# Attention scores in three f32r passes instead of one f32 matmul, with q split on ScalarE and VectorE

## The chip, the cores and the metric

The kernel runs on one core of one Trainium2 chip. The metric is the device time of one execution in microseconds; smaller is better.

## The reference

The input x has 2 sequences of 2048 tokens with 512 values each, and ctx has 2 x 77 tokens of 512. The layer is a cross attention followed by a feed forward part, each with a residual:

```
xn = layernorm(x)
q, k, v = xn @ Wq.T + bq, ctx @ Wk.T + bk, ctx @ Wv.T + bv      # 16 heads of 32
scores = q k^T / sqrt(32), with key s masked for token t where s > t
x = x + (softmax(scores) @ v) @ Wo.T + bo
xn = layernorm(x)
gate, up = fp4(xn) @ fp4(w_gate).T, fp4(xn) @ fp4(w_up).T        # 1408 values each
x = x + fp4(silu(gate) * up) @ fp4(w_down).T
```

`fp4` takes blocks of 16 values, scales each to its largest and rounds to the grid 0, 0.5, 1, 1.5, 2, 3, 4, 6 and back. All inputs are float32, and the rounding to the grid makes the result sensitive to small errors ahead of it. So most products are made with split operands: a high half that f32r (a rounded float32 that TensorE takes in one pass) holds exactly, and a low half that is the rest. `split_matmuls` (L170 to L178) adds high x high, high x low and low x high.

## The kernel before

A tile is 128 tokens; there are 32. The kernel has two stages, attention for all tiles, then feed forward for all tiles, and no engine needs another core. Each of the five engines has its own program; they meet through semaphores, whose waits are written out by hand, and so is the order of steps on each engine. Nothing is planned at run time: an engine that waits holds up all that stands behind it in its program.

In the attention stage, `iteration(a, n)` stands once for each engine. It works on tile a and the two before it (a - 1, a - 2), and beside them on one of 33 pieces n of the feed forward weights: it is rounded to fp4, turned and split there, 11 pieces of w_gate, 11 of w_up (kept in SBUF as `wguh`, `wgul`), and 11 of w_down, which go to DRAM through the outgoing buffer `wd_out`. Pieces from number 3 on are turned by DMA: SyncE's queue transposes the grid values (`grid_transposed`, L497), stores the block scales (L491), loads them back spread over partitions with eight DMAs (`scales_in`, L504), and GpSimd multiplies (`scale_turned`, L586). `piece_high` on ScalarE (L867) and `piece_low` on VectorE (L1028) split the result. `store_piece` (L485) sends a down piece away, after `scales_in` in the order of SyncE's queue. Before, `wd_out` has two places, and a new piece waits for the store of the last but one.

Order of the steps around the change, in one iteration:

- TensorE: q of tile a in 12 f32r passes (`project_q`), transposes of att, probabilities, q and xn, the output matmuls of tile a - 2 in 12 passes, the scores of tile a, probabilities times v of tile a - 1, one transpose of scales.
- ScalarE: copy of q (L850), high half of att (L844), copies of the turned probabilities (L881), `shift` of piece n (L146), high half of xn (L888), 16 exps with the negative maxima as bias (L898), `piece_high`, rows of scales (L873).
- VectorE: largest of each block, low half of att (L963), scale, inverse and negative inverse of the piece, `q_bias` (L970), `piece_low`, rounding of the piece (L151, L155), low half of xn, grid values (L1033), residual (L982), maxima of the scores (L990), norm statistics, normalised att, normalised x (L1017).
- GpSimd: division of the piece (L140), `scale_turned`, norm scalars, addition of the output bias (L570).

The scores of a tile are 16 heads of 77 keys in three PSUM banks. The keys stand in `kbd` as a block diagonal of four heads, so five matmuls do, of 4, 2, 2, 4 and 4 heads: 308, 154, 154, 308 and 308 columns, in plain f32 with `qt`, the turned q with its bias, as the stationary operand (L764). A first tile of a sequence adds the mask with a bf16 matmul ahead of each.

The first tile and the setup (all before about 50 us) are written out: Wk, Wq, Wv, Wo are loaded and turned, `keys()` on VectorE fills `kbd` with eight steps on 32 partitions (L1112), `values` makes `vext` (v with a column of ones), and SyncE's queue places it in the block diagonal `vbd` with 24 DMAs (L538), before it goes on to the pieces.

## Time and profile before

| | us |
|---|---|
| median of 3 runs | 1179.34 (1178.81 to 1179.55) |
| time of the profiled execution | 1178.53 |
| its span | 1176.7 |
| TensorE matmuls busy | 1158.8 (98%) |
| VectorE busy | 970.3 (82%) |
| ScalarE busy | 483.5 (41%) |
| GpSimd busy | 179.3 (15%) |
| granted TensorE clock, mean | 0.999 |

The span goes from the first to the last instruction of the profiled execution; its own time has 1.8 us around that. Times in the trace count from the start of the span. A row in order of time has the start, the duration, the engine, the line of the kernel, the operation, output and inputs by name, shapes, and how many instructions are merged in it; in brackets stands idle time of the engine before it and what ended it. PE is TensorE, PEld its weight loads, DVE VectorE, ACT ScalarE, POOL GpSimd, SPq the queue of SyncE. Matmuls overlap each other in the pipeline, so a busy TensorE isn't at its peak, and start to start is the measure of its pace. A plain f32 matmul shows as two records, an f32r pass as one. Rows of DMA issues show the time of the issue; the landing comes later.

### The profile page before, as it was taken

To read this page: it belongs to the slowest core of one execution; us is meant where nothing else is said; L and a number is where in the kernel's file an instruction comes from. 1 tells how busy PE (TensorE), PEld (TensorE's weight loads), DVE (VectorE), ACT (ScalarE), POOL (GpSimd) and SP (SyncE) were. 2 spreads that over 40 slices of the span, in tenths; PEclk is the share of its full clock that TensorE was granted. 3 is DMA by queue.
4 is the path that set the end of the run, shared out by engine and by line. 5 is a ranking of instruction groups with operands and counts; after the bars stand their busy time and mean duration, and the time that the engine had idled before them with its cause. 6 is when DMAs were issued, how large, how long until landed. Compare 5 with 4: busy or idle time off the path is not lost.

```text
span 1176.7 us, 21716 instructions
## 1 busy us (share of the span) xinstructions
PE 1158.8 (98%) x6784; PEld 1057.6 (90%) x6784; DVE 970.3 (82%) x1609; ACT 483.5 (41%) x1201; POOL 179.3 (15%) x305
## 2 busy tenths in 40 slices
PE   7899999999999999999999999999999999999998
PEld 6688888888888889999999999999999999999997
DVE  6778888888888877988888888888888888888865
ACT  3556656566566553333332332233233323333321
POOL 3433333333333310000000000000000000000000
PEclk9999999999999999999999999999999999999999
DMA  7223323323344436554445345444534454453442
GB/s 240 45 89 88 111 88 110 91 84 111 108 139 148 132 108 194 150 105 86 89 89 102 70 93 99 88 88 87 105 70 93 98 90 88 82 104 76 82 85 46
DMA packets 154955, 119.30 MB, mean 101 GB/s; under 512 B 95597, under 2 KB 122301, under 8 KB 154660
## 3 DMA queue, kind: packets, MB, share of 16 engines
q1 hardware_dynamic: 154916, 118.85, 42.7%
q8 instruction: 16, 0.26, 0.1%
q14 instruction: 23, 0.19, 0.1%
HBM read 74.47 MB, written 24.94 MB: 84 GB/s over the span
## 4 chain that ended last, share of the span: by engine, by line
PE 78%; SPq 7%; DMA 7%; DVE 2%; ACT 2%; issue 2%; POOL 2%; POOLq 0%; DVEq 0%; ACTq 0%
PE g_ps L175 7%; PE u_ps L175 7%; PE u_ps L176 7%; PE g_ps L176 7%; PE u_ps L177 7%; PE g_ps L177 7%; PE d_ps L1436 6%; PE d_ps L1437 6%; PE d_ps L1435 6%; SPq L504 4%; DMA ws_dram<-w_rows 4%; PE o_ps L784 3%; PE s_ps L764 3%; DMA w_wide<-ws_dram 3%; POOL w_q L586 2%
## 5 line engine op out<-in xcount | busy, mean ns | idle before, releaser
L175 PE MATMUL g_ps<-wguh,xnh 128*128 128x352 f32 x496 | 162.4, 327 | 0.5 <-issue 0.5
L175 PE MATMUL u_ps<-wguh,xnh 128*128 128x352 f32 x496 | 159.9, 322 | 0.5 <-DVE hid L1576 0.5
L176 PE MATMUL u_ps<-wgul,xnh 128*128 128x352 f32 x496 | 159.8, 322 | 0.0
L176 PE MATMUL g_ps<-wgul,xnh 128*128 128x352 f32 x496 | 159.8, 322 | 0.0
L177 PE MATMUL u_ps<-wguh,xnl 128*128 128x352 f32 x496 | 159.6, 322 | 0.0
L177 PE MATMUL g_ps<-wguh,xnl 128*128 128x352 f32 x496 | 159.5, 322 | 0.0
L898 ACT ACTIVATE probs<-s_ps,nsmax 128x77 f32<-128x77 f32 x512 | 113.7, 374 | 92.2 <-DVE nsmax L990 92.2
L1576 DVE TENSOR_TENSOR hid<-u_ps,silu 128x352 f32<-128x352 f32 x128 | 66.8, 522 | 78.1 <-PE u_ps L177 75.8
L1437 PE MATMUL d_ps<-wd,hql 128*128 128x512 f32 x330 | 128.9, 391 | 0.0
L1436 PE MATMUL d_ps<-wd,hqh 128*128 128x512 f32 x330 | 128.9, 391 | 0.0
L1435 PE MATMUL d_ps<-wd,hqh 128*128 128x512 f32 x330 | 128.4, 389 | 0.0
L1478 ACT ACTIVATE silu<-g_ps 128x352 f32<-128x352 f32 x128 | 58.4, 460 | 134.0 <-PE g_ps L177 134.0
L274 POOL TENSOR_TENSOR nmean<-f_mv,minus_one 128x1 f32<-128x1 f32 x32 | 6.1, 190 | 630.8 <-DVE f_mv L269 630.8
L175 PEld LDWEIGHTS g_ps<-wguh,xnh 128*128 128x128 f32 x496 | 93.1, 188 | 2.6 <-issue 0.9
L146 ACT ACTIVATE quant_magic<-quant_z 128x512 bf16<-128x512 f32 x65 | 41.0, 631 | 132.2 <-DVE quant_z L140 79.5
L176 PEld LDWEIGHTS g_ps<-wgul,xnh 128*128 128x128 f32 x496 | 93.2, 188 | 1.1
L175 PEld LDWEIGHTS u_ps<-wguh,xnh 128*128 128x128 f32 x496 | 93.1, 188 | 0.8 <-DVE hid L1576 0.8
L177 PEld LDWEIGHTS u_ps<-wguh,xnl 128*128 128x128 f32 x496 | 93.4, 188 | 0.0
L177 PEld LDWEIGHTS g_ps<-wguh,xnl 128*128 128x128 f32 x496 | 93.4, 188 | 0.0
L176 PEld LDWEIGHTS u_ps<-wgul,xnh 128*128 128x128 f32 x496 | 93.2, 188 | 0.0
L784 PEld LDWEIGHTS o_ps<-vbd,probsT 128*128 128x128 f32 (+1 forms) x640 | 76.5, 191 | 4.4
L784 PE MATMUL o_ps<-vbd,probsT 128*128 128x66 f32 (+2 forms) x640 | 75.0, 272 | 0.0
(175 smaller groups left out, 2547.1 us busy)
## 6 DMA issues: line engine op xcount, KB each, us to landing
scale_wide<-st_dram SPq DMA_DIRECT2D x248, 88.0 KB, 3.4
xin<-in_x_dram SPq DMA_DIRECT2D x32, 256.0 KB, 2.8
x_dram<-x SPq DMA_DIRECT2D x32, 256.0 KB, 2.2
xin<-x_dram SPq DMA_DIRECT2D x32, 256.0 KB, 2.7
out_dram<-y SPq DMA_DIRECT2D x32, 256.0 KB, 2.1
scale_wide<-st_dram SPq DMA_DIRECT2D x248, 32.0 KB, 1.8
w_wide<-ws_dram SPq DMA_DIRECT2D x240, 32.0 KB, 1.9
wd_dram<-wd_out SPq DMA_DIRECT2D x11, 512.0 KB, 3.0
```

The costliest lines, as they stand in the source:

```text
L146: s.activation(self.magic[:, part.cols], self.z[:, part.cols], ACT.Copy, scale=ULP_SHIFT).then_inc(self.shifted_ready, 1)
L175: pe.matmul(out, lh, rh, start=(i == 0), stop=False)
L176: pe.matmul(out, lh, rl, start=False, stop=False)
L177: last = pe.matmul(out, ll, rh, start=False, stop=(i == n - 1))
L504: sp.dma_start(w_wide[b * BLK:(b + 1) * BLK, :, :], ws_dram[:, b, :].unsqueeze(0).to_broadcast([BLK, EC, P])).then_inc(w_wide_loaded, 16)
L784: last = pe.matmul(o_ps[:, half, h0 * VW:(h1 + 1) * VW], probsT[0:rows, i, :], vbd[0:rows, b, half, c, 0:(h1 - h0 + 1) * VW], start=(c == ...
L898: last = act.activation(probs[:, h * CTX:(h + 1) * CTX], s_ps[:, bank, o:o + CTX], ACT.Exp, bias=nsmax[:, h:h + 1], scale=1.0)
L1435: pe.matmul(total, high[:, c, :], wd[:, 0, c, :], start=(c == 0), stop=False)
L1436: pe.matmul(total, high[:, c, :], wd[:, 1, c, :], start=False, stop=False)
L1437: summed = pe.matmul(total, low[:, c, :], wd[:, 0, c, :], start=False, stop=(c == FC - 1))
L1478: act.activation(silu[:, c % 2, :], g_ps[:, c % 2, 0:GU_N], ACT.Silu).then_inc(silu_ready, 1)
L1576: dve.tensor_tensor(hid[:, c * GU_N:(c + 1) * GU_N], u_ps[:, c % 2, 0:GU_N], silu[:, c % 2, :], ALU.mult).then_inc(hid_ready, 1)
```

## The change

The keys are kept as a high and a low half, `kbh` and `kbl`, and q as `qh` and `ql`, all f32r. Each of the five score matmuls becomes three passes. On ScalarE, `q_high` makes the high half in four biased copies of 128 columns out of PSUM, after the copies of the turned probabilities and ahead of `shift`. On VectorE, `q_low` makes the low half in four steps, and stands behind `piece_low`, where `q_bias` stood ahead of it. TensorE waits for both. In the setup VectorE makes the whole keys `kf` in one step, ScalarE copies them into `kbh` in eight steps ahead of the first q copy, and VectorE subtracts in eight steps to `kbl` ahead of the first `q_low`. The places of both must be zeroed, one more memset on GpSimd. In SBUF, `wd_out` has one place, `vext` and `kf` lie in rows that only the setup uses, and q lies under `ql`.

```diff
-        kbd = sb("kbd", [P, B, EC, 4 * CTX])
+        kbh, kbl = sb("kbh", [P, B, EC, 4 * CTX], F32R), sb("kbl", [P, B, EC, 4 * CTX], F32R)
...
-        q = sb("q", [P, E])
-        qt = sb("qt", [P, EC, P])
+        with ExitStack() as qctx:
+            q = qctx.enter_context(nc.sbuf_tensor("q", [P, E], F32))
+        ql = sb("ql", [P, EC, P], F32R)
+        qh = sb("qh", [P, EC, P], F32R)
...
-        wd_out = sb("wd_out", [P, 2, 2, E], F32R)
+        wd_out = sb("wd_out", [P, 2, E], F32R)
...
-            pool.memset(kbd[:], 0.0).then_inc(zeroed, 1)
+            pool.memset(kbh[:].bitcast(F32), 0.0).then_inc(zeroed, 1)
+            pool.memset(kbl[:].bitcast(F32), 0.0).then_inc(zeroed, 1)
...
             def scores(a):
-                pe.wait_ge(q_ready, a + 1)
+                pe.wait_ge(qh_ready, a + 1)
+                pe.wait_ge(ql_ready, a + 1)
...
-                    last = pe.matmul(out, qt[:, c, :], kbd[:, b, c, (h0 % 4) * CTX:(h0 % 4 + h1 - h0) * CTX],
-                                     start=not causal, stop=True)
+                    cols = slice((h0 % 4) * CTX, (h0 % 4 + h1 - h0) * CTX)
+                    pe.matmul(out, qh[:, c, :], kbh[:, b, c, cols], start=not causal, stop=False)
+                    pe.matmul(out, qh[:, c, :], kbl[:, b, c, cols], start=False, stop=False)
+                    last = pe.matmul(out, ql[:, c, :], kbh[:, b, c, cols], start=False, stop=True)
...
+            def q_high(t):
+                act.wait_ge(qT_done, t + 1)
+                if reached(t):
+                    act.wait_ge(s_done, S_BANKS * t)
+                for c in range(EC):
+                    last = act.activation(qh[:, c, :], q_ps[:, c * P:(c + 1) * P], ACT.Identity, bias=bqc[:, c:c + 1], scale=1.0)
+                last.then_inc(qh_ready, 1)
...
                 if down:
                     c = n - GU_PIECES
-                    if isinstance(c, int) and c >= 2:
-                        act.wait_ge(wd_stored, 16 * (c - 1))
-                    if not isinstance(c, int):
-                        act.wait_ge(wd_stored, 16 * (c - 1))
-                    dst = wd_out[:, c % 2, 0, :].rearrange("p (c k) -> p c k", k=P)
+                    if reached(c):
+                        act.wait_ge(wd_stored, 16 * c)
+                    dst = wd_out[:, 0, :].rearrange("p (c k) -> p c k", k=P)
...
                 if valid(a - 1):
                     probs_copy(a - 1)
+                if valid(a):
+                    q_high(a)
...
+            def keys():
+
+                act.wait_ge(kf_ready, 1)
+                act.wait_ge(zeroed, 2)
+                for b in range(B):
+                    for i in range(4):
+                        r = slice(i * HD, (i + 1) * HD)
+                        last = act.activation(kbh[r, b, :, i * CTX:(i + 1) * CTX], kf[r, :, b * CTX:(b + 1) * CTX], ACT.Copy)
+                last.then_inc(kbh_ready, 1)
...
             wquant.shift(act, 1)
+            keys()
             q_copy(0)
             weight_high(2)
+            q_high(0)
...
-            def q_bias(t):
-                dve.wait_ge(qT_done, t + 1)
+            def q_low(t):
+                dve.wait_ge(qh_ready, t + 1)
                 if reached(t):
                     dve.wait_ge(s_done, S_BANKS * t)
-                dve.tensor_tensor(qt[:], q_ps[:].rearrange("p (c k) -> p c k", k=P), bcast(bqc[:], P), ALU.add).then_inc(q_ready, 1)
+                for c in range(EC):
+                    last = dve.scalar_tensor_tensor(out=ql[:, c, :], in0=q_ps[:, c * P:(c + 1) * P], scalar=bqc[:, c:c + 1],
+                                                    in1=qh[:, c, :].bitcast(F32), op0=ALU.add, op1=ALU.subtract)
+                last.then_inc(ql_ready, 1)
...
-                if valid(a):
-                    q_bias(a)
                 if by_dma(n - 2):
                     piece_low(n - 2, down)
+                if valid(a):
+                    q_low(a)
...
-                for b in range(B):
-                    for i in range(4):
-                        r = slice(i * HD, (i + 1) * HD)
-
-                        last = dve.scalar_tensor_tensor(
-                            out=kbd[r, b, :, i * CTX:(i + 1) * CTX],
-                            in0=kp[r].rearrange("p a (c s) -> p (a c) s", c=2)[:, :, b * CTX:(b + 1) * CTX],
-                            scalar=SCALE, in1=bcast(bkc[r, :], CTX), op0=ALU.mult, op1=ALU.add)
-                last.then_inc(kbd_ready, 1)
+                dve.scalar_tensor_tensor(out=kf[:], in0=kp[:].rearrange("p a (c s) -> p (a c) s", c=2)[:, :, 0:B * CTX],
+                                         scalar=SCALE, in1=bcast(bkc[:], B * CTX), op0=ALU.mult,
+                                         op1=ALU.add).then_inc(kf_ready, 1)
+
+            def keys_low():
+
+                dve.wait_ge(kbh_ready, 1)
+                for b in range(B):
+                    for i in range(4):
+                        r = slice(i * HD, (i + 1) * HD)
+                        cols = slice(i * CTX, (i + 1) * CTX)
+                        last = dve.tensor_tensor(kbl[r, b, :, cols], kf[r, :, b * CTX:(b + 1) * CTX],
+                                                 kbh[r, b, :, cols].bitcast(F32), ALU.subtract)
+                last.then_inc(kbl_ready, 1)
...
             piece_rounded(0)
-            q_bias(0)
+            keys_low()
+            q_low(0)
             piece_scales(1)
```

## Rows read from the trace of the kernel before

**Rows 1.** Busy us (x instructions) by window: PE, PEld, DVE, ACT, POOL; clock, DMA, GB/s.
```profile
92.00:240.00 148.00, 147.76 (x926) 129.09 (x925) 126.56 (x267) 91.46 (x305) 50.97 (x61) 1.00 0.33 98
...
290.00:414.00 124.00, 124.00 (x774) 108.69 (x773) 104.90 (x220) 77.39 (x254) 42.57 (x53) 1.00 0.43 134
```

**Rows 2.** Waits, 60 to 430 us: total us, times, longest.
```profile
ACT q L850 <- PE q_ps L177: 4.1, 14, 1.0
```

**Rows 3.** The chain that ended last, 300 to 327 us, by line.
```profile
by line: DMA ws_dram<-w_rows 22.5%; DMA w_wide<-ws_dram 21.6%; SPq L504 21.3%; SPq L497 13.4%; POOL w_q L586 13.1%; issue 6.4%; SPq L463 3.9%; SPq L457 3.1%; SPq L477 2.9%; POOLq L585 0.4%; POOLq L563 0.2%; SPq L496 0.2%; SPq L462 0.1%; SPq
```

**Rows 4.** TensorE in order of time, 209 to 213 us: start us, us, engine, line.
```profile
208.99 2.24 PE L764 MATMUL s_ps<-kbd,qt 128*128 128x308 f32 x10
211.07 2.34 PE L784 MATMUL o_ps<-vbd,probsT 128*128 128x66 f32 x20
```

**Rows 5.** ScalarE in order of time, 89 to 102 us.
```profile
89.18 3.56 ACT L898 ACTIVATE probs<-s_ps,nsmax 128x77 f32<-128x77 f32 x16 [2.95 <-DVE nsmax L990]
...
94.14 1.37 ACT L881 ACTIVATE probsT<-s_ps 128x512 f32<-128x512 f32 x3
...
97.19 0.63 ACT L146 ACTIVATE quant_magic<-quant_z 128x512 bf16<-128x512 f32 x1 [1.69 <-POOL quant_z L140]
...
101.26 3.12 ACT L898 ACTIVATE probs<-s_ps,nsmax 128x77 f32<-128x77 f32 x14 [2.95 <-DVE nsmax L990]
```

**Rows 6.** VectorE in order of time, 94 to 98 us.
```profile
94.38 0.69 DVE L963 TENSOR_TENSOR atl<-w_ps,ath 128x512 fp32r<-128x512 f32 x1 [1.08 <-ACT ath L844]
...
95.58 0.18 DVE L134 TENSOR_SCALAR quant_ninv<-quant_inv 128x32 f32<-128x32 f32 x1
95.77 0.69 DVE L970 TENSOR_TENSOR qt<-q_ps,bqc 128x512 f32<-128x512 f32 x1
96.38 1.33 DVE L1028 TENSOR_TENSOR wgul<-w_q,wguh 128x512 f32 x1
97.86 0.29 DVE L151 TENSOR_SCALAR quant_magic<-quant_magic 128x512 int16<-128x512 int16 x1
```

**Rows 7.** GpSimd, then VectorE, in order of time.
```profile
83.48 1.61 POOL L140 TENSOR_TENSOR quant_z<-w_in,quant_ninv 128x512 f32<-128x512 f32 x1 [3.00 <-DVE quant_ninv L134]
...
96.10 1.06 POOL L140 TENSOR_TENSOR quant_z<-w_in,quant_ninv 128x512 f32<-128x512 f32 x1 [1.99 <-DVE quant_ninv L134]
...
83.49 0.68 DVE L1028 TENSOR_TENSOR wgul<-w_q,wguh 128x512 f32 x1
```

**Rows 8.** TensorE in order of time, 620 us: f32r passes of 352 columns.
```profile
620.11 0.32 PE L177 MATMUL u_ps<-wguh,xnl 128*128 128x352 f32 x1
...
620.27 0.32 PE L175 MATMUL u_ps<-wguh,xnh 128*128 128x352 f32 x1
```

**Rows 9.** The line that stores down pieces; ScalarE in order of time.
```profile
L485 SPq DMA_DIRECT2D wd_dram<-wd_out x11: 520/538/638, 311.7 to 431.1; - x11
DMA to landing us min/median/max: 3.0/3.0/4.6
...
314.70 0.66 ACT L867 ACTIVATE wd_out<-w_q 128x512 f32 x1
```

**Rows 10.** The start, in order of time: VectorE, ScalarE, TensorE, SyncE's queue, GpSimd.
```profile
19.74 3.90 DVE L1112 SCALAR_TENSOR_TENSOR kbd<-kp,bkc 32x308 f32<-32x308 f32 x8 [0.45 <-PE kp L670]
...
20.46 0.63 ACT L146 ACTIVATE quant_magic<-quant_z 128x512 bf16<-128x512 f32 x1 [4.28 <-POOL quant_z L140]
22.53 0.60 ACT L850 ACTIVATE q<-q_ps 128x512 f32<-128x512 f32 x1 [1.43 <-PE q_ps L177]
23.02 2.06 ACT L940 ACTIVATE wvt<-tp 128x512 f32<-128x512 f32 x4
...
25.14 3.66 PE L679 MATMUL o_ps<-wvt,ctxT 128*77 128x512 f32 x8 [0.36 <-ACT wvt L940]
...
29.67 20.57 SPq L538 DMA_DIRECT2D vbd<-vext  x24
...
9.05 0.19 POOL L564 TENSOR_TENSOR veps<-mv,eps 128x1 f32<-128x1 f32 x1 [3.30 <-DVE mv L1011]
```

More of the change, by code:

```diff
@@ L200, in __init__ @@
             self.wkt, self.wvt = row(("wkt", [P, EC, E]))[0], row(("wvt", [P, EC, E]))[0]
-            self.cin, self.ctxT = row(("cin", [CTX, B, E]), ("ctxT", [P, EC, B, CTX]))
-            self.bv_all, self.bias_nat = row(("bv_all", [CTX, E]), ("bias_nat", [EC, 2, P]))
+            self.cin, self.ctxT, self.kf = row(("cin", [CTX, B, E]), ("ctxT", [P, EC, B, CTX]), ("kf", [P, EC, B * CTX]))
+            self.bv_all, self.bias_nat, self.vext = row(
+                ("bv_all", [CTX, E]), ("bias_nat", [EC, 2, P]), ("vext", [CTX, B, 2, HALF_HEADS, VW]))
 class Shared:
@@ L354, in attention @@
         mask = sb("mask", [P, CTX], BF16)
-        vext = sb("vext", [CTX, B, 2, HALF_HEADS, VW])
         wqh, wql = sb("wqh", [P, EC, E], F32R), sb("wql", [P, EC, E], F32R)
@@ L377, in attention @@
         w_nat, wkt, wvt, cin, ctxT = k.setup.w_nat, k.setup.wkt, k.setup.wvt, k.setup.cin, k.setup.ctxT
-        bv_all, bias_nat = k.setup.bv_all, k.setup.bias_nat
+        bv_all, bias_nat, vext, kf = k.setup.bv_all, k.setup.bias_nat, k.setup.vext, k.setup.kf
         with ExitStack() as sctx:
@@ L405, in attention @@
         small_done, small_ready = sem("small_done"), sem("small_ready")
-        k_done, kbd_ready = sem("k_done"), sem("kbd_ready")
+        k_done, kf_ready, kbh_ready, kbl_ready = sem("k_done"), sem("kf_ready"), sem("kbh_ready"), sem("kbl_ready")
         v_done, v_ready = sem("v_done"), sem("v_ready")
@@ L415, in attention @@
         xnT_done, xnh_ready, xnl_ready = sem("xnT_done"), sem("xnh_ready"), sem("xnl_ready")
-        q_done, q_copied, qT_done, q_ready = sem("q_done"), sem("q_copied"), sem("qT_done"), sem("q_ready")
+        q_done, q_copied, qT_done, qh_ready, ql_ready = (sem(n) for n in (
+            "q_done", "q_copied", "qT_done", "qh_ready", "ql_ready"))
         s_done, nsmax_ready, probs_ready = (sem(n) for n in ("s_done", "nsmax_ready", "probs_ready"))
@@ L484, in store_piece @@
                     sp.wait_ge(wd_stored, 16 * c)
-                sp.dma_start(wd_dram[:, :, c, :], wd_out[:, c % 2].bitcast(F32)).then_inc(wd_stored, 16)
+                sp.dma_start(wd_dram[:, :, c, :], wd_out[:].bitcast(F32)).then_inc(wd_stored, 16)
             def scales_out(n):
@@ L530, in sp_part @@
             sp.wait_ge(const_ready, 3)
-            sp.wait_ge(zeroed, 2)
+            sp.wait_ge(zeroed, 3)
             for b in range(B):
@@ L685, in project_q @@
                 if reached(a):
-                    pe.wait_ge(q_ready, a)
+                    pe.wait_ge(qh_ready, a)
+                    pe.wait_ge(ql_ready, a)
                 else:
@@ L754, in scores @@
                 if not reached(a):
-                    pe.wait_ge(kbd_ready, 1)
+                    pe.wait_ge(kbh_ready, 1)
+                    pe.wait_ge(kbl_ready, 1)
                 b = a // TB
@@ L1023, in piece_low @@
                     c = n - GU_PIECES
-                    high, low = (wd_out[:, c % 2, i, :].rearrange("p (c k) -> p c k", k=P) for i in range(2))
+                    high, low = (wd_out[:, i, :].rearrange("p (c k) -> p c k", k=P) for i in range(2))
                 else:
@@ L1105, in keys @@
                 dve.wait_ge(k_done, 1)
-                dve.wait_ge(zeroed, 1)
                 dve.wait_ge(small_ready, 3)
+                dve.scalar_tensor_tensor(out=kf[:], in0=kp[:].rearrange("p a (c s) -> p (a c) s", c=2)[:, :, 0:B * CTX],
[3 more added lines that the diff above has]
+                dve.wait_ge(kbh_ready, 1)
                 for b in range(B):
@@ L1175, in dve_part @@
             run(dve, iteration, 1)
-        over = Over(q_done, q_ready, pT_ready, att_ready, wo_done, x1_ready, xb_ready)
+        over = Over(q_done, ql_ready, pT_ready, att_ready, wo_done, x1_ready, xb_ready)
         return Parts(sp_part, pool_part, pe_part, act_part, dve_part), over
```

## Prediction

> **What bounds the kernel now.** I read the busy times by window first. The change lies in the attention stage, which ends at about 430 us of 1176.7. There TensorE is listed as busy all the time, VectorE 85%, ScalarE 62%, GpSimd 34% [rows 1]. One tile makes 77 matmul records (12 for q, 12 for the output, 10 scores, 20 probabilities by v, 23 transposes). So 926 records in 148 us are 12.0 tiles of about 12.33 us, and 774 in 124 us are 10.05 of the same 12.33.
>
> A full TensorE is not yet a TensorE that bounds, so I looked for loops that return to themselves without it. There are two, and both are nearly as long.
>
> The first I call the vector loop: exps, piece high, rows of scales, q copy and high half of att on ScalarE; low half of att, then scale, inverse and its negative on VectorE; division on GpSimd; shift on ScalarE; rounding, residual and maxima on VectorE; exps again. From 89.18 to 101.26 it takes 12.08 us [rows 5]. Its one steady wait for TensorE, at the q copy, is only 4.1 us in 14 cases over 370 us, some 30 tiles [rows 2]; this tile has none. So this loop has about 0.25 us of slack against 12.33.
>
> The second I call the transfer loop: transposed grid, store, loads, scales out and landed, eight scale loads and landed, GpSimd's product, next transpose. In the stage of the down pieces the chain that ended last runs through it almost alone: scales out 22.5%, scales in 21.6%, their issues 21.3%, transpose 13.4%, GpSimd's product 13.1% [rows 3]. There a faster TensorE buys nothing.
>
> **The change, part by part.**
>
> *Scores.* Before, the ten records of the five f32 matmuls take from 208.99 to 211.07, 2.08 us for 1232 columns, 1.69 ns a column [rows 4]. After, each of the five is three f32r passes: nine of 308 columns and six of 154. The nearest f32r row is 352 columns at 0.16 us from start to start [rows 8]; at full speed, 2.4 GHz, the columns are 0.147 of it, so 0.013 is overhead. A pass of 308 is then 0.141. For 154 no f32r row exists. Bounds: the same arithmetic gives 0.077; the f32 rate of rows 4 gives 0.26. I take 0.11, which is what one of the 20 short records of probabilities by v takes (2.18 us in all, up to the next piece: 2.34 less the overlap of about 0.16 that the scores' row shows too) [rows 4]. Sum: 9 x 0.141 + 6 x 0.11 = 1.93, saving 0.15 a tile. Ends: 1.73 (saves 0.35) and 2.83 (costs 0.75). TensorE's own loop becomes 12.18 us.
>
> *q's halves.* ScalarE is free at 94.14 + 1.37 = 95.51 and shifts at 97.19 [rows 5]; the four biased copies go in there. A step of 77 columns with a bias costs 3.56 / 16 = 0.22 [rows 5], one of 512 columns 2.06 / 4 = 0.51 [rows 10]. I take 0.28 for 128 columns (nearer to the 77), so 1.1 to 1.2 for four, with ends 0.9 and 2.0: the high half is there at 96.7. That is within the hole. VectorE had its bias step at 95.77 and the piece's low half at 96.38 [rows 6]; the two change places. Four low steps start at 96.75. One costs between 0.2 (the 0.18 us step of 32 columns [rows 6] with its gap) and 0.49 (3.90 / 8 for 308 columns [rows 10]). I take 0.26, near the low end because only 128 columns stream, so 1.05 for four: ready at 97.8, with 0.8 and 2.0 as ends. The rounding waits for ScalarE's shift at 97.86 anyway [rows 6], so the four steps are covered by 0.1 to 0.3 us, no more. Behind them on VectorE stand rounding, xn low, residual and maxima, and all ScalarE waits for the maxima. TensorE's twelve output matmuls begin when att's low half is there, at 94.38 + 0.69 [rows 6], and take 12 x (0.213 + 0.013) = 2.7, so to 97.8: the scores hardly wait.
>
> *The low half of the piece comes earlier, and that has a price.* At 96.38 it took 1.33 us because GpSimd was dividing; where it began within 0.01 us of the division it took 0.68 and GpSimd needed 1.61 instead of 1.06 as at 96.10, ending at 85.09, 0.92 after VectorE's step ended at 84.17 [rows 7]. Now the step starts at 95.77, 0.3 us ahead of GpSimd's 96.10, and ends at 96.46. By the same 0.92 the division ends at 97.38; before, it ended just ahead of the shift at 97.19 [rows 5]. So shift and rounding move by 0.22 us, and the vector loop goes from 12.08 to 12.30. Bounds: nothing (the division is not held up), or 0.55 (it is held up in full).
> The Trainium skill ("SBUF — State Buffer", the section on the engine ports) says VectorE and GpSimd share a port pair that is an exclusive lock for the whole instruction for two-SBUF-input steps, whoever starts first. Rows 7 agree in both directions (1.33 and 1.61). By it the hand-over cannot be free, which speaks against the change.
> The Trainium skill ("ScalarE: Activation LUTs", what ACT_TABLE_LOAD costs) adds 93 ns for each pointer operand; by its figures an estimate for the four copies is 1.27 us instead of 1.2. No row has 128 columns with a bias.
>
> So for tiles 4 to 20: TensorE 12.18, vector loop 12.30, transfers just below. The largest is 12.30 against 12.33: 16 x 0.03 = 0.5 us gained, practically nothing. TensorE's saving goes into the wait of the output matmuls for att's low half.
>
> *One outgoing buffer.* It touches 10 of the 11 down pieces. The store is issued after the eight scale loads, the first one at 311.7, and lands 3.0 us later (4.6 at worst), that is at 314.7; the next piece's high half now writes the same buffer and started at 314.70 [rows 9]. Until now it had a tile more. So landing and need fall together. I price one late landing of 4.6 at 1.0 and the rest at 0.05 each: 1.5 us, ends 0 and 3. Behind this wait on ScalarE stand the scale rows and the q copy, then att's high half, for which VectorE and TensorE wait. In that stage the transfer loop sets the pace, so TensorE's gain gives nothing back.
>
> *The start.* VectorE's eight key steps (3.90 us from 19.74 [rows 10]) become one of 616 columns (about 0.8, by 0.49 for 308) and eight subtractions (3.2 to 3.9). ScalarE gets eight copies of 308 columns ahead of the q copy: 0.34 each (between 0.22 and 0.51), 2.7 us, and they can't begin before the shift ends at 20.46 + 0.63 = 21.09. So the q copy goes from 22.53 to 23.75, wv's copies and the value matmuls (25.14) follow by 1.2 [rows 10]. VectorE can begin the subtractions at 23.8; with the low half of q and the next scales it arrives at the values at about 30.1. SyncE's queue of 24 placements of v, 20.57 us long, starts at 29.67 as soon as v is there [rows 10], and moves by 1.2 too. I add 0.2 for tile 1, where the halves of q are late for TensorE by about 1 us before it has slack: 1.4, ends 0.5 and 2.5. A second memset of 2 us on GpSimd lies in the 3.3 us that it idles before 9.05 [rows 10] and costs nothing; without that cover it would be 2. New places of vext and kf in memory cost nothing.
>
> Sum: +1.4 - 0.5 + 1.5 = +2.4, and the first score tile -0.1, gives +2.3. On the profiled execution (span 1176.7, time 1178.53) that is 1180.8; the median of the runs is 0.8 above it, 1179.34, so 1181.6.
>
> **The rivals.**
> *A. TensorE's gain passes through.* The lock costs nothing and ScalarE's copies at the start hide behind the wait for TensorE. Then 32 x 0.15 = 4.8 us come off, 1174.5. For it: TensorE busy 100%. Against it: rows 3, and a slack of only 0.25. It decides if the vector loop stays below 12.18.
> *B. Narrow passes don't get the f32r rate.* Six of 154 columns at 0.26: scores take 2.83, TensorE's loop 13.08, 32 x 0.75 = +24 us, 1203. For it: no f32r row under 352 columns in the trace. Against it: short f32 records go at 0.11. It decides from 0.135 a narrow pass (scores no cheaper than 2.08).
> *C. The small steps cost more.* 0.1 us more for each of the eight: the low half is there at 98.6 instead of 97.8, 0.5 after the shift, vector loop 12.8; 27 tiles x 0.47 = +12.7, 1194. It decides when both sets together pass 98.1. For it: thin cover; against: rows of short steps (0.18 to 0.22).
> *D. The change doesn't do what it says*: nothing in the code speaks for that; the third pass is there in each group.
>
> **How the numbers follow.** The forecast and what lies close around it (1178 to 1186, by the ends of start, landing and lock) gets 0.55, A 0.2, B 0.13, C 0.12. A change of under 0.2%, 2.4 us, can't be told from none here. The forecast lies at that edge, so its 0.55 goes 0.28 to no change and 0.27 to slower. Faster: A, 0.2. Slower: B, C and the rest, 0.52. The range takes in A and most of C and leaves B out: 1174.5 to 1192.
>
> **What would show it.** Fifteen score records a tile, spanning 1.9 us; a pass of 154 columns near 0.11. The low half of the piece at 0.7 and GpSimd's division at 1.3. VectorE idle less than 0.3 before the rounding. TensorE waiting before the output matmuls. ScalarE waiting for the store in some down pieces. Tiles of 12.3 us in both windows, and v's placements from about 31. The forecast is wrong if tiles are under 12.2 or over 12.5, or if the start moves by more than 2.5.

## The result, and the profile after

| | before | changed |
|---|---|---|
| median, us | 1179.27 (1178.81 to 1182.34, 8 runs) | 1188.3 (1184.23 to 1189.33, 8 runs) |
| profiled execution, its span | 1178.53, 1176.7 | 1188.65, 1186.7 |
| TensorE, VectorE busy | 1158.8, 970.3 | 1164.4, 974.8 |
| ScalarE, GpSimd busy | 483.5, 179.3 | 516.6, 189.6 |
| mean granted clock | 0.999 | 0.992 |

The ratio is 1.0066, with a 95% interval of 1.005 to 1.0082: slower, by 9.0 us in the medians and 10.1 between the profiled executions. The forecast said slower by 2.3, and its range held the time.

The loss is spread very unevenly. This table follows fixed points of the program through both traces, in us from the start of the span:

| point | before | changed | later by |
|---|---|---|---|
| first maxima of tile 0 | 32.16 | 35.20 | 3.0 |
| q copy, tile 1 | 45.24 | 48.73 | 3.5 |
| first score, tile 1 | 48.13 | 52.85 | 4.7 |
| q copy, tile 2 | 55.66 | 64.79 | 9.1 |
| q copy, tile 3 | 67.91 | 76.97 | 9.1 |
| q copy, last tile | 414.38 | 423.68 | 9.3 |
| first gate group of the FFN | 427.76 | 437.48 | 9.7 |

So 9.1 of some 10 us are lost before 65 us, and the 29 tiles after that lose next to nothing. Half of the 9.1 is lost in one tile, and there TensorE's clock is the thing to look at. Busy time by window of the changed kernel, with the columns of [rows 1]; the column of one number behind POOL is the granted clock:

```profile
42.30:45.70 3.40, 3.40 (x11) 2.83 (x12) 2.54 (x6) 1.11 (x2) 1.83 (x2) 0.50 0.11 16
45.70:52.60 6.90, 4.38 (x29) 3.27 (x27) 3.55 (x10) 3.83 (x10) 2.12 (x2) 0.99 0.12 17
52.60:62.80 10.20, 9.95 (x41) 9.60 (x42) 7.10 (x16) 4.47 (x19) 1.35 (x3) 0.50 0.28 70
62.80:73.00 10.20, 10.20 (x71) 9.30 (x69) 6.09 (x15) 4.80 (x13) 2.89 (x3) 1.00 0.09 26
92.00:240.00 148.00, 148.00 (x986) 133.56 (x986) 124.96 (x301) 101.57 (x350) 55.36 (x61) 1.00 0.32 97
290.00:414.00 124.00, 123.42 (x823) 111.51 (x823) 104.51 (x252) 85.19 (x291) 45.08 (x51) 1.00 0.42 129
```

From 42.3 to 45.7 and from 52.6 to 62.8 the clock was the lower of its two levels, 1.2 GHz. The kernel before had it only from 11.3 to 14.7; the changed one has that early stretch too, from 11.6 to 15.0. In the second stretch TensorE is busy 9.95 of 10.20 us and gets through 41 records; the next 10.20 us hold 71. Ahead of the stretch it was busy 4.38 of 6.90 us. In the two lower windows, 986 records against 926 in rows 1: tiles have 82 records instead of 77, and the clock is full.

TensorE in order of time: tile 1 of the kernel before, then of the changed kernel tile 1 and a later tile at full clock.

```profile
48.13 2.35 PE L764 MATMUL s_ps<-kbd,qt 128*128 128x308 f32 x10 [1.15 <-DVE qt L970]
...
49.87 0.60 PE L747 MATMUL xn_ps<-ident,xn 128*128 128x128 f32 x4
52.85 0.59 PE L773 MATMUL s_ps<-kbh,qh 128*128 128x308 f32 x1 [2.39 <-DVE ql L1001]
53.24 0.46 PE L774 MATMUL s_ps<-kbl,qh 128*128 128x308 f32 x1
...
56.58 4.37 PE L794 MATMUL o_ps<-vbd,probsT 128*128 128x66 f32 x20
...
217.40 0.30 PE L773 MATMUL s_ps<-kbh,qh 128*128 128x308 f32 x1
217.54 0.30 PE L774 MATMUL s_ps<-kbl,qh 128*128 128x308 f32 x1
217.69 0.31 PE L775 MATMUL s_ps<-kbh,ql 128*128 128x308 f32 x1
217.83 0.23 PE L773 MATMUL s_ps<-kbh,qh 128*128 128x154 f32 x1
...
218.24 0.28 PE L774 MATMUL s_ps<-kbl,qh 128*128 128x154 f32 x1
218.35 0.27 PE L775 MATMUL s_ps<-kbh,ql 128*128 128x154 f32 x1
218.46 0.34 PE L773 MATMUL s_ps<-kbh,qh 128*128 128x308 f32 x1
...
219.35 2.34 PE L794 MATMUL o_ps<-vbd,probsT 128*128 128x66 f32 x20
```

At full clock a pass of 308 columns takes 0.14 to 0.15 from start to start and one of 154 columns 0.11, and the scores 219.35 - 217.40 = 1.95 where rows 4 had 2.08. In tile 1 TensorE waits 2.39 us for q's low half, where the kernel before waited 1.15 for q, and then every record is long: 0.46 instead of 0.30, and the probabilities by v 4.37 instead of 2.34.

The middle tile of the changed kernel on ScalarE, VectorE and GpSimd, in order of time (it answers to rows 5, 6 and 7):

```profile
214.70 1.18 ACT L867 ACTIVATE qh<-q_ps,bqc 128x128 fp32r<-128x128 f32 x4
216.79 0.63 ACT L146 ACTIVATE quant_magic<-quant_z 128x512 bf16<-128x512 f32 x1 [0.92 <-POOL quant_z L140]
...
213.72 0.69 DVE L993 TENSOR_TENSOR atl<-w_ps,ath 128x512 fp32r<-128x512 f32 x1 [1.12 <-ACT ath L854]
...
215.15 0.69 DVE L1061 TENSOR_TENSOR wgul<-w_q,wguh 128x512 f32 x1
216.01 1.13 DVE L1001 SCALAR_TENSOR_TENSOR ql<-q_ps,bqc,qh 128x128 fp32r<-128x128 f32 x4 [0.17 <-ACT qh L867]
217.46 0.29 DVE L151 TENSOR_SCALAR quant_magic<-quant_magic 128x512 int16<-128x512 int16 x1 [0.32 <-ACT quant_magic L146]
...
215.34 1.42 POOL L140 TENSOR_TENSOR quant_z<-w_in,quant_ninv 128x512 f32<-128x512 f32 x1 [1.88 <-DVE quant_ninv L134]
```

The four copies take 1.18, the four low steps 1.13. The piece's low half is down from 1.33 to 0.69, and GpSimd's division is up from 1.06 to 1.42. VectorE idles 0.32 before the rounding. The next tile begins 12.33 later, as do nearly all tiles beside which a piece of w_gate or w_up is worked on; before, they alternated between 12.30 and 12.35. In the stage of the down pieces the tiles take 12.2 to 12.8. Of the waits of the changed kernel from 75 to 440 us:

```profile
ACT q L860 <- PE q_ps L177: 0.5, 2, 0.3
...
ACT wd_out L883 <- DMA wd_dram<-wd_out: 0.8, 3, 0.4
```

The first answers to rows 2: from there on the q copy hardly waits for TensorE now (3.8 us in 13 cases in the same window before). The vector loop has no slack left and sets the pace. The second is what ScalarE waits for the single outgoing buffer: 0.8 us in three pieces, where it waited 0.2 in one before. TensorE's saving turns into a wait, as forecast: in the tile above, its output matmuls start 0.51 us after the transposes of xn ahead of them (214.04 to 214.55), before it was 0.36 (205.77 to 206.13).

The start of the changed kernel, ScalarE and then VectorE (rows 10):

```profile
20.98 3.77 ACT L967 ACTIVATE kbh<-kf 32x308 fp32r<-32x308 f32 x8
24.77 0.60 ACT L860 ACTIVATE q<-q_ps 128x512 f32<-128x512 f32 x1
25.27 2.06 ACT L958 ACTIVATE wvt<-tp 128x512 f32<-128x512 f32 x4
...
19.76 0.80 DVE L1141 SCALAR_TENSOR_TENSOR kf<-kp,bkc 128x616 f32<-128x616 f32 x1 [0.49 <-PE kp L675]
...
24.78 3.87 DVE L1152 TENSOR_TENSOR kbl<-kf,kbh 32x308 fp32r<-32x308 f32 x8 [1.93 <-ACT kbh L967]
28.68 1.13 DVE L1001 SCALAR_TENSOR_TENSOR ql<-q_ps,bqc,qh 128x128 fp32r<-128x128 f32 x4
29.73 0.68 DVE L120 TENSOR_REDUCE quant_amax<-w_in 128x32 f32<-128x512 f32 x1
...
31.20 0.68 DVE L1161 TENSOR_TENSOR vext<-o_ps,bv_all 77x512 f32<-77x512 f32 x1
...
33.13 0.69 DVE L151 TENSOR_SCALAR quant_magic<-quant_magic 128x512 int16<-128x512 int16 x1 [0.29 <-ACT quant_magic L146]
...
35.20 1.56 DVE L1023 TENSOR_REDUCE nsmax<-s_ps 128x6 f32<-128x462 f32 x3
```

The last three of these steps in the kernel before:

```profile
28.90 0.69 DVE L1123 TENSOR_TENSOR vext<-o_ps,bv_all 77x512 f32<-77x512 f32 x1 [0.82 <-PE o_ps L679]
...
30.50 0.28 DVE L151 TENSOR_SCALAR quant_magic<-quant_magic 128x512 int16<-128x512 int16 x1
...
32.16 1.56 DVE L990 TENSOR_REDUCE nsmax<-s_ps 128x6 f32<-128x462 f32 x3
```

A key copy on ScalarE takes 0.47, and VectorE idles 1.93 for them. The step that makes v comes 2.3 later than before, the rounding 2.6 later, and the rounding takes 0.69 instead of 0.28, so that the maxima come 3.0 later.

### The profile page after: what moved, and what is told of

Same layout as the page of the kernel before. It is cut to its first block, busy times and chain, and to the rows that moved or that the text cites. A ratio compares the mean times of both kernels' runs of the same rounds, so it can differ in the third digit from the quotient of the medians.

```text
span 1186.7 us, 22287 instructions
## 1 busy us (share of the span) xinstructions
PE 1164.4 (98%) x6944; PEld 1073.5 (90%) x6944; DVE 974.8 (82%) x1706; ACT 516.6 (44%) x1337; POOL 189.6 (16%) x306
## 4 chain that ended last, share of the span: by engine, by line
PE 85%; DVE 3%; DMA 3%; ACT 3%; SPq 2%; issue 2%; POOL 1%; DVEq 0%; POOLq 0%; ACTq 0%
PE g_ps L175 7%; PE u_ps L175 7%; PE u_ps L176 7%; PE g_ps L176 7%; PE u_ps L177 7%; PE g_ps L177 7%; PE d_ps L1475 6%; PE d_ps L1476 6%; PE d_ps L1474 6%; PE o_ps L794 4%; PE s_ps L735 2%; PE w_ps L175 2%; PE q_ps L175 2%; PE w_ps L177 2%; PE w_ps L176 2%
```

## The experiments

Eleven kernels, each timed in five rounds against the kernel before. They ran in three groups; the kernel before had medians of 1179.92, 1180.57 and 1181.54 over the runs up to each, so the ratio is the measure, not the time alone. The two numbers behind a ratio are its 95% interval.

**One outgoing buffer, alone.** (e1_one_outgoing_buffer) The kernel before with one edit:

```diff
-        wd_out = sb("wd_out", [P, 2, 2, E], F32R)
+        wd_out = sb("wd_out", [P, 2, E], F32R)
...
+                    if reached(c):
+                        act.wait_ge(wd_stored, 16 * c)
```

> The kernel before with one outgoing buffer for the down pieces, and nothing else of the change. Theory (my term for it): a store lands when the next piece wants the buffer, so 1.5 us more, 0 to 3, ratio 1.000 to 1.0025, and one to three waits of ScalarE for the store in the stage of the down pieces. Rival: the single buffer carries a good part of the 9 us by which the changed kernel is slower: then 4 us or more, ratio over 1.0034.

Measured: 1180.78 us (1178.30 to 1181.63), ratio 1.000 [0.9989, 1.0011]. The profile has a span of 1177.6 against 1176.7, and ScalarE waits 1.0 us in all for the store (0.2 before). So the buffer costs between nothing and about 1 us.

**Two passes instead of three.** (e2_two_passes) The changed kernel without the product of q's high half with the keys' low half:

```diff
-                    pe.matmul(out, qh[:, c, :], kbl[:, b, c, cols], start=False, stop=False)
```

> The changed kernel with the pass qh x kbl left out of the scores, so five f32r passes a tile fewer; about 0.65 us less work for TensorE a tile, 20 us over 32 tiles. Theory (the vector loop sets the pace): the tiles in the middle stay at 12.33 us, the whole time falls by under 2 us, and TensorE waits about 0.65 us more a tile ahead of the output matmuls. Rival (TensorE sets it): tiles of 11.7 us, some 20 us less, about 1168.

Measured: 1187.18 (1185.38 to 1189.44), ratio 1.0067 [1.0052, 1.0082]. A third of the score passes is gone, and the time and the tiles of 12.33 us stay. In the middle of the attention stage TensorE isn't the limit any more.

**Idle matmuls in tile 1.** (e3_filler_matmuls) The changed kernel, with TensorE's waits of tile 1 filled by f32r passes whose result nobody reads:

```diff
+            def filler(n):
+                for _ in range(n):
+                    pe.matmul(w_ps[:], wqh[:, 0, 0:P], wqh[:, 1, :], start=True, stop=True)
...
                 if isinstance(a, int) and a == 1:
+                    pe.wait_ge(wth_ready, 4 * EC)
+                    pe.wait_ge(wtl_ready, 2 * EC)
+                    filler(8)
                     transpose_piece(2)
...
+                if isinstance(a, int) and a == 1:
+                    filler(10)
                 if valid(a):
                     scores(a)
```

> The changed kernel with 18 idle f32r matmuls of 512 columns, whose result nobody reads, in the two gaps that TensorE has in tile 1 (8 ahead of the turning of piece 2, 10 ahead of the scores). Theory: about 5 of the 9 us by which the changed kernel is slower are matmuls at 1.2 GHz between 52.4 and 62.7 us, after those gaps; with the gaps filled the granted clock is 0.999 in each run, and the median is 1183 to 1185. Rival: the late vector chain of the start costs the 9 us by itself: 1187 to 1189 as before.

Measured: 1186.02 (1183.18 to 1188.38), ratio 1.0055 [1.0039, 1.007]. The window from 52 to 58 us of its profile:

```profile
52.00:58.00 6.00, 5.90 (x41) 5.21 (x40) 5.22 (x14) 3.05 (x11) 1.06 (x1) 1.00 0.22 63
```

The long stretch at half clock is gone (the one at 42 isn't). The scores of tile 1 come 1.4 us later, because the filling is longer than the gap, and yet the q copy of tile 2 comes at 61.55 instead of 64.79. The median falls by 2.3 (by the ratios it is 1.3), less than the 3 to 5 that I expected, and the interval overlaps that of the changed kernel: the profile shows the effect, the times alone don't.

**Scales ahead of the key steps.** (e4_scales_first) The changed kernel, with one line moved in VectorE's start:

```diff
+            piece_scales(1)
             keys_low()
             q_low(0)
-            piece_scales(1)
```

> The changed kernel with the scales of piece 1 on VectorE moved ahead of the low half of the keys, into the 1.93 us in which VectorE waits for ScalarE's key copies. Theory (the start is bound by VectorE's chain): the first maxima come 1.4 us earlier, at 33.8 instead of 35.2, and the time falls by 1.4 us in runs of the same clock. Rival (the start is bound by ScalarE's copies and the value matmuls behind them): no change at the first exps.

Measured: 1183.72 (1182.04 to 1185.65), ratio 1.0035 [1.0022, 1.0047]. First maxima at 34.28 (35.20), first exps at 35.25 (35.86), exps of tile 1 at 54.34 (55.66). So 0.9 us is gained at the maxima, where 1.4 was expected, and 1.3 only in tile 1. The median is 4.6 lower (by the ratios 3.7), more than the 1.4 expected; this profile's stretch at half clock is 6.8 us instead of 10.2. Part of the gain is paid back: the key subtractions took 5.61 us instead of 3.87, beside GpSimd's division (1.22) and its addition of the output bias (1.50), which now run at the same time.

**The piece's low half first, alone.** (e5_low_first_alone) The kernel before, with the two steps exchanged on VectorE:

```diff
-                if valid(a):
-                    q_bias(a)
                 if by_dma(n - 2):
                     piece_low(n - 2, down)
+                if valid(a):
+                    q_bias(a)
```

> The kernel before with one edit: the low half of the piece ahead of the bias of q on VectorE. Theory (the lock on the shared port moves the division): GpSimd's division goes from 1.06 to 1.4, rounding comes 0.2 to 0.35 later, and the vector loop goes from 12.08 to about 12.35. TensorE's own loop is still 12.33 here, so a tile stays at 12.33 to 12.4 and the time rises by 0 to 2 us, ratio 1.000 to 1.0017, but the q copy no longer waits for TensorE. Rival (the division is not held up, or the loop has slack enough): division 1.06, no change at all.

Measured: 1181.73 (1180.62 to 1185.25), ratio 1.0009 [0.9999, 1.002]. GpSimd's division in its profile:

```profile
145.29 1.34 POOL L140 TENSOR_TENSOR quant_z<-w_in,quant_ninv 128x512 f32<-128x512 f32 x1 [1.97 <-DVE quant_ninv L134]
```

So the order alone makes the division 0.28 longer. Middle tiles are 12.35 (12.33), those of the down stage 12.48 (12.33).

**The piece's low half earlier still.** (e6_low_early) The changed kernel: outside the down stage the low half goes ahead of att's low half, well before the division, and GpSimd adds the output bias one tile later, out of its way. The edit to that addition isn't shown here.

```diff
...
+                if by_dma(n - 2) and not down:
+                    piece_low(n - 2, down)
                 if valid(a - 2):
                     att_low(a - 2)
...
-                if by_dma(n - 2):
+                if by_dma(n - 2) and down:
                     piece_low(n - 2, down)
```

> The changed kernel; outside the stage of the down pieces the low half of the piece stands ahead of att's low half, in VectorE's idle 1.1 us, and the addition of the output bias on GpSimd is made one tile later, behind the scaled product, so that it does not hold the port there. Theory (the lock costs the vector loop 0.25 to 0.35 us a tile): the division is back at 1.06, and tiles of the middle go from 12.33 to about 12.2 (TensorE's own 12.19), 16 x 0.13 = 2 us less than the changed kernel. Rival (something else holds 12.33, as the transfers): division at 1.06, but tiles stay at 12.3 and the time as it is.

Measured: 1187.64 (1184.61 to 1191.93), ratio 1.006 [1.0041, 1.008]. GpSimd's division and two starts of ScalarE's exps in its profile:

```profile
138.59 1.06 POOL L140 TENSOR_TENSOR quant_z<-w_in,quant_ninv 128x512 f32<-128x512 f32 x1 [3.83 <-DVE quant_ninv L134]
...
143.75 3.57 ACT L918 ACTIVATE probs<-s_ps,nsmax 128x77 f32<-128x77 f32 x16 [2.95 <-DVE nsmax L1027]
155.93 3.35 ACT L918 ACTIVATE probs<-s_ps,nsmax 128x77 f32<-128x77 f32 x15 [2.95 <-DVE nsmax L1027]
```

The division is back at 1.06 and the tile at 12.18, which is TensorE's own loop of the prediction. But one tile in about seven takes 12.8: in the one from 180.30 to 193.18 GpSimd's product waits 5.00 us for the scale loads, and VectorE idles 1.17 for the norm scalars that stand behind it. That fits a transfer loop slower than 12.18 that asks for its time back. No gain in the median is shown: the interval is nearly that of the changed kernel.

**Short key steps.** (e7_short_keys) The changed kernel with only one of the eight key copies and one of the eight subtractions; the other seven blocks of the keys are left at zero, so most of the scores are left out. The same edit stands in both places:

```diff
-                    for i in range(4):
+                    for i in range(1 - b):
```

> The changed kernel with one of the eight key copies on ScalarE and one of the eight subtractions on VectorE; the other seven blocks of the keys are left at zero. Theory (the start is lost in these 7 x 0.47 + 7 x 0.48 us): first maxima 4 to 5 us earlier than in the changed kernel, by 31 us, and the time is within 1.5 us of the kernel before or below it, 1177 to 1181, with no stretch of half clock after 50 us. Rival (the loss is in the loop or in tile 1's later halves of q): over 1184.

Measured: 1186.46 (1184.69 to 1188.95), ratio 1.0045 [1.0028, 1.0061]. The first exps came at 33.53, only 0.6 behind the kernel before. I had expected 1177 to 1181 and no half clock behind 50 us. My theory that the loss lies in the key steps fell here, because in tile 1 the old loss came back in full:

```profile
49.70:60.00 10.30, 9.92 (x41) 9.57 (x42) 7.24 (x17) 4.61 (x19) 1.32 (x3) 0.50 0.27 72
```

The scores of tile 1 again begin after a wait of 2.40 us for q's low half, at half clock, and the q copy of tile 2 stands at 62.00, 6.3 behind the kernel before. What is left when the start is repaired is the wait in tile 1.

**The start mended.** (e8_start_mended) The changed kernel with the scales first, key steps merged over both batches, and twelve idle matmuls in tile 1 (five and seven):

```diff
-                for b in range(B):
-                    for i in range(4):
+                for i in range(4):
+                    r = slice(i * HD, (i + 1) * HD)
+                    last = act.activation(kbh[r, :, :, i * CTX:(i + 1) * CTX],
+                                          kf[r].rearrange("p c (b s) -> p b c s", b=B), ACT.Copy)
```

> The changed kernel with three edits of the start: scales of piece 1 ahead of the low keys, the key steps on ScalarE and VectorE merged from eight of 308 columns to four of 616, and 12 idle matmuls in the two gaps of tile 1 (5 and 7). Theory (the whole loss is the start and the clock behind it): four steps of 616 columns cost 0.7 and 0.8 us, 0.9 and 0.7 less in all; granted clock 0.998 or more, ratio to the kernel before 1.001 to 1.003, about 1182. Rival (the clock falls anyway, or the fillers cost what they save): 1184 or more, as with the scales moved alone.

Measured: 1184.78 (1181.23 to 1185.35), ratio 1.0025 [1.0014, 1.0036]. No stretch at half clock in its profile, q copy of tile 2 at 58.85 (64.79) and the FFN at 432.55 (437.48). Of the 0.66% of the change, 0.41 come back, some 4.8 us.

**Both mended.** (e9_both_mended) The edits of the last one and of the early low half together; no new lines.

> The changed kernel with the mended start of e8_start_mended (scales of the next piece ahead of the key steps, four key copies and four subtractions of 616 columns, twelve idle f32r matmuls in tile 1) and with the early low half of the piece of e6_low_early (it goes ahead of att's low half outside the down stage, and the bias add one tile later). If the two losses are separate they add: e8 alone measured a ratio of 1.0025 to the kernel before, e6 alone 1.0060 against 1.0066 for the change, and in e6's profile the last q copy came about 1.5 to 2 us earlier by its shorter tiles (12.18 against 12.33, with one of 12.8 in seven). Theory (start and middle are separate): ratio 1.0005 to 1.0020, some 1181.5 to 1183, with the FFN starting at about 430.5 to 431.5 in the profile. Rival (the transfer loop takes back what the tiles gain): the same as e8, 1.0025, FFN at 432.5.

Measured: 1183.94 (1182.05 to 1185.43), ratio 1.0019 [1.0007, 1.0031], FFN at 432.34. The ratio is at the upper end of the theory, the profile is the rival's. At the q copy of tile 4 this kernel is 2.5 us behind the kernel before (82.73 against 80.26), and at that of the last tile 4.1 (418.52 against 414.38): the shorter tiles don't make up for the start, they lose some more. Tiles of 12.18 alternate with some of 12.7 to 13.2, and one of the down stage takes 14.06. The intervals of this and the last kernel overlap, so that the early low half gains anything on top isn't shown. It is the best version of the change that I have, and still slower than the kernel before.

**A late q in the kernel before.** (e10_late_q) This measures the disputed mechanism without any of the change. Seven idle VectorE steps in tile 1, which write a spare buffer:

```diff
...
+                if isinstance(a, int) and a == 1:
+                    for i in range(7):
+                        dve.tensor_scalar(spare[:, i, :], wquant.scale[:], 1.0, None, ALU.mult)
                 if valid(a):
                     q_bias(a)
```

> The kernel before, with nothing changed but seven idle VectorE steps of 32 columns (0.18 us each, about 1.3 in all) ahead of q's bias step in tile 1. There TensorE already waits 1.15 us for q before the scores of tile 1; now it waits about 2.4, as in the changed kernel. VectorE itself has 1.24 us of idle time behind that step, so its own loop is hardly late. Theory (the gap ahead of the scores of tile 1 is what lets the granted clock fall, whatever causes it): the profile shows a stretch at half clock that begins 4 to 8 us after 48, the q copy of tile 2 moves from 55.66 to 60 or later, and the median is 3 to 6 us above the kernel before, ratio 1.0025 to 1.005. Rival (the changed kernel's clock fell because of its f32r passes or its later start, not because of the gap): no half clock after 15 us, q copy of tile 2 at 56 to 57, ratio up to 1.001.

Measured: 1184.89 (1182.85 to 1187.83), ratio 1.0034 [1.0019, 1.0048]. TensorE in order of time:

```profile
46.92 0.60 PE L742 MATMUL xn_ps<-ident,xn 128*128 128x128 f32 x4
50.13 4.03 PE L765 MATMUL s_ps<-kbd,qt 128*128 128x308 f32 x10 [2.61 <-DVE qt L971]
54.00 2.34 PE L785 MATMUL o_ps<-vbd,probsT 128*128 128x66 f32 x20
```

**The same, with TensorE kept busy.** (e11_late_q_filled) As the last one, with five and seven idle matmuls in the waits.

> e10_late_q, and in the same tile TensorE fills its waits with twelve idle f32r matmuls of 512 columns (five ahead of the transposes of piece 2, seven ahead of the scores, 0.23 us each). The same delay of q, but without idle TensorE. Theory (the clock is the price, the delay itself is nearly free): full clock in the profile after 15 us, q copy of tile 2 at 56 to 57.5, ratio 1.000 to 1.0015. Rival (the delay costs by itself, by the queues behind it): as e10.

Measured: 1181.69 (1179.41 to 1182.96), ratio 1.0004 [0.9995, 1.0013], q copy of tile 2 at 56.45.

```profile
46.13 1.84 PE L685 MATMUL w_ps<-wqh 128*128 128x512 f32 x7
48.99 2.35 PE L769 MATMUL s_ps<-kbd,qt 128*128 128x308 f32 x10 [1.02 <-DVE qt L980]
51.18 2.34 PE L789 MATMUL o_ps<-vbd,probsT 128*128 128x66 f32 x20
```

Both delay q by the same 1.5 us: from the first q copy to the scores of tile 1 it is 27.07 us in either (23.06 to 50.13, 21.92 to 48.99), 25.60 in the kernel before. With TensorE idle for 2.61 us the clock was half from 50.2 to 53.6, the scores took 4.03 instead of 2.35, and the kernel is 0.34% slower. With the wait filled the scores take 2.35 and the kernel can't be told from the one before. The two intervals don't touch, so it is shown that the idle TensorE costs, and that the delay alone costs little. The stretch was 3.4 us here, not the 10.2 of the changed kernel, and the q copy of tile 2 came at 59.27 where I had said 60 or later.

That all of the 0.3% goes through the clock isn't shown. Counted from the first q copy, that of tile 2 comes after 36.21 us with TensorE idle, 34.53 with the wait filled and 33.13 in the kernel before: 1.4 for the delay, 1.7 for the half clock. The profiles differ by another 2.5 from the q copy of tile 4 to that of the last tile (337.7 against 335.2 us, 334.1 before), where neither has half clock, and the other profiles spread from 333.7 to 337.4 there. And the mean granted clock of the single executions doesn't sort their times well: the three of the late q with 0.999 or 1.000 took 1182.85, 1184.14 and 1186.49, the five below that 1184.38 to 1187.83, and two of the three lie above every filled one (at most 1182.96). A stretch of 3.4 us at half clock would bring the mean to some 0.9986 (an estimate: 1.7 of 1184 us), so the one with 1.000 had none. The same wait isn't always followed by half clock.

## Why the prediction was right or wrong

*The middle tiles: right.* Forecast 12.30, measured 12.33. The score passes cost what was worked out (1.95 against 1.93, a narrow pass 0.11 against 0.11), so rival B is out. The four copies (1.18) and low steps (1.13) are within 0.1 of their terms, so C is out. GpSimd's division went to 1.42 where I had 1.28, and with it the last 0.03 of gain went away. That TensorE's saving turns into a wait can be seen three times: its output matmuls start 0.15 later behind the transposes, the q copy waits 0.5 us for TensorE instead of 3.8, and two passes are no faster than three. Rival A fell for the reason given against it. With VectorE's low half and GpSimd's bias addition both moved away from the division, tiles drop to 12.18. So what held them at 12.33 was the vector loop with its longer division; which of the two moves shortened it wasn't separated.

*One outgoing buffer: too dear.* 1.5 forecast; about 0 to 1 measured. In the changed kernel the landings were 3.0 to 3.4 us after the issue, not the 4.6 for which I had put 1.0; with the edit alone one took 4.6 again, and ScalarE still waited only 1.0 in all.

*The start: mis-sized.* 1.2 forecast for it, 3.0 measured at the first maxima. The first 1.0 that was missing is ScalarE's: a key copy took 0.47 and not 0.34, so the q copy came at 24.77 instead of the 23.75 forecast, and v 2.3 later than before instead of 1.2. That VectorE can't begin the subtractions before the copies are there was in the prediction, and so was that the next scales stand behind them. What waits for those scales was not: GpSimd's division starts at 31.37 instead of 28.16 and ScalarE's shift at 32.47 instead of 29.76, so the rounding comes another 0.3 later, and it took 0.4 longer, beside GpSimd's addition of the output bias. Moving the scales forward gave 0.9 back at the maxima and 1.3 in tile 1.

*Tile 1: the step that failed.* The prediction put it as "I add 0.2 for tile 1, where the halves of q are late for TensorE by about 1 us before it has slack". The lateness was right: from the q copy to the first score it is 52.85 - 48.73 = 4.12 instead of 48.13 - 45.24 = 2.89, so 1.2 more. What I left out was that TensorE already stood still there for 1.15 us, that the wait becomes 2.39, and that the clock it is granted afterwards depends on it. From the first score of tile 1 to the q copy of tile 2 it is 11.94 us instead of 7.53: 4.4 us more, for a stretch of 10.2 us at half clock, which would lose 5.1 if TensorE were the only limit. Nothing in the sum had the clock in it, although the profile before shows one such stretch (11.3 to 14.7), behind the idle start.

The account at the q copy of tile 2, in one line: 3.0 for the start, 0.5 up to the q copy of tile 1, 1.2 for the halves of q, 4.4 behind them, together 9.1; then 0.2 to the last tile and 0.4 to the FFN. That half clock can follow an idle TensorE in the kernel before too is shown by e10 and e11. That it made up the 4.4 in the profiled execution of the changed kernel is shown by e3: from the first score of tile 1 to the q copy of tile 2 it is 61.55 - 54.24 = 7.3 us there, as in the kernel before (7.5). For the medians the share of the clock is less sure. Filling the waits alone brought 2.3 us that are not clear of the scatter, moving the scales alone 4.6, and both with merged key steps 0.41% of the 0.66%.

*The spread.* The eight executions of the changed kernel range over 5.1 us. Mean granted clock and time go together, loosely: two with 0.999 took 1184.8 and 1185.7, the four with 0.995 or less 1187.9 to 1189.3, and two with 0.997 took 1184.2 and 1189.2. How long a stretch at half clock gets differs from kernel to kernel with the same wait of about 2.4 to 2.6 us ahead of it (3.4, 6.8 and 10.2 us in the profiles). What decides the length stays open, and so does the stretch at 42.3 to 45.7: ahead of it TensorE idled 1.68 and 0.73 us with 1.1 us of work between, while the kernel with two passes idled 1.87 and 0.70 there and kept the full clock.

*By its own signs.* The prediction named what would show it wrong: tiles under 12.2 or over 12.5, or a start that moves by more than 2.5. The tiles held, but for single ones of the down stage (up to 12.80), and the start did not: it moved by 3.0 at the first maxima and 9.1 at the q copy of tile 2. The placements of v began at 32.9, not near 31. The time of 1188.3 also lies above the 1178 to 1186 given for the forecast and what lies close around it. It fell inside the wide range because that made room for rival C at 1194, whose small steps in the loop didn't happen. That the range held is luck.

*What it says of the centre.* The sum said 2.3 more for the profiled execution, and it was 10.1. Of the 7.8 between them the clock in tile 1 is 4.4, and the start with the halves of q in tile 1 is 3.3 (4.7 instead of 1.4). All that lies behind the q copy of tile 2 was forecast at 0.9 (-0.5, +1.5 and -0.1) and measured at 1.0. That agreement is chance as well: the 1.0 is 0.2 up to the last tile, 0.4 up to the FFN and 0.4 behind it, for which the sum has no term.

## What to carry to other kernels

Before making a consumer of TensorE's work later by a microsecond, look how long TensorE already waits there: here 1.15 us of idle time was harmless, and 2.4 to 2.6 was followed by half clock in all six profiles that had it, which cost 4.4 us in the profile of the changed kernel and 1.7 in that of the late q. Where such a wait can't be taken away, useless matmuls in it can be worth their place; with the late q they turned 0.34% into 0.04%, in the changed kernel what they bring in the median is within the scatter. And a saving on TensorE counts only up to the next loop: price that loop first, with the instruction pairs that hold each other up on VectorE and GpSimd.

## What the runs showed of the hardware

- In the profiles the granted clock fell to its lower level, 1.2 GHz, after a wait of TensorE of 2.4 to 2.6 us ahead of the scores of tile 1: for 10.2 us in the changed kernel and with short keys, 6.8 with two passes and with the scales first, 3.4 with the early low half and the late q. It did not fall after 0.8 to 1.15 in the same place (the kernel before, one outgoing buffer, low half first, the mended start, both mended, the late q filled). One execution of the late q with a mean clock of 1.000 shows that the fall doesn't come every time.
- An f32r pass of 154 columns takes 0.11 us from start to start, one of 308 columns 0.14 to 0.15.
- A step of VectorE with two SBUF inputs that starts just ahead of GpSimd's division lengthens the division from 1.06 to 1.34 (alone) and 1.42 us (in the change); eight key subtractions beside that division and the bias addition took 5.61 us instead of 3.87. In the first two cases VectorE's step had 0.42 and 0.50 us still to run when the division began, and the division took 0.28 and 0.36 longer. This agrees in kind with the Trainium skill ("SBUF — State Buffer", the section on the engine ports): whoever starts first holds the shared ports.
- Copies of 32 x 308 from SBUF to SBUF on ScalarE took 0.47 us each; four of 32 x 616 took 2.92, 0.73 each. Merging eight into four saves 0.85 us.
